# Computing the chosen two of eight experts, with rows sorted by expert through memory

## The reference, cut to what matters

```python
gate = softmax(flat_x @ w_gate.T)                    # flat_x = layernorm(x)
topk_scores, topk_idx = top_k(gate, 2)               # of 8 experts
cw = (one_hot(topk_idx, 8) * topk_scores[..., None]).sum(axis=1)
h = gelu(einsum('td,edh->teh', flat_x, W1) + b1)     # 128 -> 512, exact gelu
y = einsum('teh,ehd->ted', h, W2) + b2               # 512 -> 128
out = einsum('ted,te->td', y, cw)                    # x = x + 0.5 * out
```

## Time and profile before

| | us |
|---|---|
| median of 3 runs (range) | 2918.71 (2918.47 to 2922.16) |
| the profiled execution, its own time | 2922.81 |
| its span, first to last instruction | 2921.0 |
| busy: PE, DVE, ACT, POOL | 2432.8, 2039.1, 1732.1, 880.6 |

### The profile page before, as it was taken

How to read it: one execution, slowest core, us unless ns; L and a number is a source line. 1 busy time by engine, 2 the same in 40 slices (tenths; PEclk the granted TensorE clock), 3 DMA queues, 4 the chain that set the end, 5 groups by cost and what they waited for, 6 DMA issues and landing times. The chain is left out here.

```text
span 2921.0 us, 55825 instructions
## 1 busy us (share of the span) xinstructions
PE 2432.8 (83%) x17750; PEld 1732.7 (59%) x17878; DVE 2039.1 (70%) x3370; ACT 1732.1 (59%) x3364; POOL 880.6 (30%) x590
## 2 busy tenths in 40 slices
PE   5999997689999937888788888787688879788878
PEld 3767764267767725666446666443566655566654
DVE  5887876667887837888457888344688845788844
ACT  4767674167767725666465666457566646566646
POOL 1222221012222205444115444110444421444411
PEclk8999998889999968999899999889899979899989
DMA  3010111010110121101001111000101100111001
GB/s 118 29 58 29 40 47 59 0 58 30 29 58 29 32 95 27 26 22 26 4 4 25 26 24 26 1 3 0 23 22 26 24 10 0 23 26 26 22 8 29
DMA packets 51706, 84.66 MB, mean 29 GB/s; under 512 B 8574, under 2 KB 15144, under 8 KB 51640
## 3 DMA queue, kind: packets, MB, share of 16 engines
q1 hardware_dynamic: 49560, 77.79, 9.6%
q0 software_dynamic: 1216, 4.20, 0.5%
q10 hardware_dynamic: 864, 1.84, 0.2%
HBM read 51.59 MB, written 2.39 MB: 18 GB/s over the span
## 5 line engine op out<-in xcount | busy, mean ns | idle before, releaser
L384 ACT ACTIVATE moe_g<-banks,b 128x512 f32<-128x512 f32 x512 | 348.2, 691 | 242.5 <-PE banks L42 228.8
L481 DVE TENSOR_TENSOR moe_gl<-moe_g,moe_gh 128x512 fp32r<-128x512 f32 x512 | 397.6, 793 | 111.9 <-ACT moe_gh L388 103.1
L1287 POOL TENSOR_TENSOR att_sums<-att_turned 128x1024 f32<-128x1024 f32 x128 | 302.8, 2365 | 368.5 <-DVE att_turned L1178 337.7
L1178 DVE TENSOR_TENSOR att_turned<-banks,tables 128x512 f32<-128x512 f32 x512 | 317.5, 683 | 44.2 <-ACT att_squares L1080 44.2
L1294 POOL TENSOR_TENSOR att_qkn<-att_sums,att_rc 128x1024 f32<-128x1024 f32 x128 | 243.9, 1906 | 266.6 <-DVE att_rc L1193 230.2
L1109 ACT ACTIVATE att_probs<-banks,att_nmax 128x128 f32<-128x128 f32 x1024 | 289.1, 375 | 14.7 <-DVE att_nmax L1203 14.7
L1203 DVE TENSOR_REDUCE att_nmax<-banks 128x4 f32<-128x512 f32 x256 | 175.3, 686 | 139.1 <-PE banks L994 132.8
L509 POOL TENSOR_TENSOR moe_acc<-moe_acc,moe_part 128x512 f32<-128x512 f32 x96 | 153.5, 1598 | 376.5 <-DVE moe_part L457 376.5
L40 PE MATMUL banks<-wqkv_h,att_hh 128*128 128x512 f32 x384 | 179.2, 467 | 103.1 <-DVE att_qt L1198 66.1
L40 PE MATMUL banks<-moe_gh,w2h 128*128 128x512 f32 x512 | 214.0, 418 | 31.3 <-DVE moe_gl L481 30.8
L40 PE MATMUL banks<-moe_xh,w1h 128*128 128x512 f32 x512 | 221.3, 432 | 20.3 <-DVE moe_xl L447 20.3
(11 more groups left out here) (232 smaller groups left out, 5656.2 us busy)
## 6 DMA issues: line engine op xcount, KB each, us to landing
moe_cwb<-cw_dram SPq DMA_DIRECT2D x144, 256.0 KB, 4.5
att_v_even<-att_v SPq DMA_DIRECT2D x224, 130.0 KB, 2.3
raw_w<-in_L_ffn_W POOLq DMA_DIRECT2D x4, 512.0 KB, 9.8
raw_w<-in_L_ffn_W POOLq DMA_DIRECT2D x8, 256.0 KB, 12.5
out<-out_tokens SPq DMA_DIRECT2D x8, 256.0 KB
raw_qkv<-in_L_ffn_wqkv SPq DMA_DIRECT2D x2, 768.0 KB, 6.6
tables<-in_rotary ACTq DMA_DIRECT2D x2, 512.0 KB
raw_gated_w<-in_L_ffn_w SPq DMA_DIRECT2D x2, 341.0 KB, 8.0
```

What stands on the lines that cost most here:

```text
L384: act.activation(g32[:, s, :], m.ps[:, UP[i % len(UP)], :], ACT.Gelu, bias=w.b1[:, i:i + 1]).then_inc(gelu_done, 1)
L481: dve.tensor_tensor(gl[:, s, :], g32[:, s, :], gh[:, s, :], ALU.subtract).then_inc(lo_done, 1)
L1178: turn = dve.tensor_tensor(turned[:, i, k, :].rearrange("q (h s j) -> q h s j", s=2, j=DH // 2), q[:, :, ::-1, :] if i else q, table.unsqu ...
L1287: pool.tensor_tensor(sums[:], turned[:, 0, :, :], turned[:, 1, :, :], ALU.add).then_inc(added, 1)
```

## The change

`moe_phase` is replaced by three phases in a row. `dispatch_phase` runs layernorm, logits and ranking for all 8 blocks, ranks each token-expert choice within its expert by small matmuls against a triangle of ones, turns the normalised tokens to one token per partition, and scatters each token row twice (once for each chosen expert) into `x_sorted` in memory, with 64 indirect transfers of 128 rows of 512 bytes that POOL issues. It ends with a table: for each tile of 128 sorted rows its expert and its first row. `experts_phase` walks 72 tiles in 9 rounds of 8: SP fetches the rows, PE turns them, and now a tile's tokens are the stationary operand and the hidden units the moving one, so `up` is three 512-column matmuls for a tile; DVE adds the bias (it lies along columns now), ACT applies gelu, PE turns the result in four pieces, ACT and DVE split it, `down` is four 256-column, four 128-column matmuls and one that adds b2, DVE writes y and SP stores it at a row that a register holds. The experts' weights are addressed by registers, which `held` reads from the table on PE, DVE and SP. `combine_phase` gathers each token's two rows with 64 indirect transfers from POOL, DVE weighs and adds them, PE turns them back, DVE adds them to x. `load_phase` also writes zeros over `x_sorted`'s spare rows and over all of `y_sorted` (35840 rows of 512 bytes, 18.35 MB, in five transfers), and spreads b1 over the partitions (2.1 MB). The phases of `ssm_phase` and later are unchanged.

```diff
+NTOK = NB * T
+TOP = 2
+TOP_ROWS = TOP * NTOK
+NTILE = 72
+FILL = 5
+GROUP = 4
+NTAB = NTILE + 2 * GROUP
+SPARE = NTAB - TOP_ROWS // P
+REGION = NTOK + P
+ROWS = NE * REGION + SPARE * P
...
+            sp.wait_ge(blanked, 3)
+            sp.dma_start(x_sorted[NE * REGION:, :].rearrange("(s p) d -> p s d", p=P), m.blank[:].unsqueeze(1).to_broadcast([P, SPARE, P])).then_inc(spare_out, 16)
+            for k in range(2):
+                sp.dma_start(raw_b2[32 * k:32 * k + 1, :], consts["b2_flat"]).then_inc(b2_in, 16)
+            sp.dma_start(w.b1[:], consts["b1_flat"].to_broadcast([P, NE * T])).then_inc(rest_in, 16)
+            wide = y_sorted.rearrange("(p f c r) d -> f p c (r d)", p=P, f=FILL, r=NB)
+            for f in range(FILL):
+                sp.dma_start(wide[f], m.x[:, NTOK:].unsqueeze(1).to_broadcast([P, ROWS // P // FILL // NB, 2 * T])).then_inc(m.y_blank, 16)
             sp.wait_ge(consts_in, 32)
-            sp.wait_ge(rest_in, 64)
+            sp.wait_ge(rest_in, 80)
+            sp.wait_ge(spare_out, 16)
...
-def moe_phase(nc, m, app, w, cw_dram):
...
+def held(nc, engine, table, lo, n, top):
+    return nc.values_load_multi_w_load_instructions(
+        table[0:1, bass.ds(lo, n)], engines=(engine,), min_val=0, max_val=top,
+        skip_runtime_bounds_check_because="the table is made of counts that the shapes bound")[1]
...
+    WAYS, XBUF = 2, 3
+    LB, XB, PB = 4, [5, 6], 7
...
+            for b in range(NB + 3):
+                if b < NB:
+                    lns[b % WAYS].centre(pe, b // WAYS, m.x[:, b * T:(b + 1) * T])
+                if 1 <= b <= NB:
+                    lns[(b - 1) % WAYS].variance(pe, (b - 1) // WAYS)
+                if 2 <= b <= NB + 1:
+                    tokens(b - 2)
+                if b >= 3:
+                    ranks(b - 3)
...
+                step(dve.tensor_tensor(pos[:], p3, base[:].unsqueeze(1).to_broadcast([P, TT, NE]), ALU.add))
+                dve.tensor_tensor(base[:], m.ps[:, PB, TT * NE:(TT + 1) * NE], base[:], ALU.add).then_inc(placed, 1)
+                step(dve.tensor_tensor(got[:], picked[:], pos[:].unsqueeze(1).to_broadcast([P, TOP, TT, NE]), ALU.mult))
+                step(dve.tensor_reduce(place[:], got[:], AX.X, ALU.add))
+                dve.tensor_copy(route.index[:, n, :, :], place[:]).then_inc(indexed, 1)
...
+            for b in range(NB + 3):
+                if 1 <= b <= NB:
+                    if b - 1 >= 2:
+                        dve.wait_ge(xt_turned, START + b - 2)
+                    lns[(b - 1) % WAYS].norm(dve, (b - 1) // WAYS, xn[:, (b - 1) % 2, :])
+                if 2 <= b <= NB + 1:
+                    gates(b - 2)
+                if b >= 3:
+                    positions(b - 3)
+                if 2 <= b <= NB + 1:
+                    select(b - 2)
+            table()
...
+            for n in range(NB):
+                pool.wait_ge(xt_kept, START + n + 1)
+                pool.wait_ge(indexed, START + n + 1)
+                for t in range(TT):
+                    for k in range(TOP):
+                        pool.indirect_dma_start(
+                            x_sorted[:, :], bass.IndirectOffsetOnAxis(ap=route.index[:, n, k, t:t + 1], axis=0),
+                            xt[:, n % XBUF, t, :], None).then_inc(scattered[n % XBUF], 16)
...
+            def up(i, q, e):
+                if q % GROUP == 0:
+                    pe.wait_ge(split, START + 2 * i + q // GROUP + 1)
+                pe.wait_ge(biased, START + ROUND * i + q - 1)
+                cols = bass.ds(e * T, T)
+                flat = lambda t: t[:].rearrange("p e t -> p (e t)")[:, cols]
+                k, t = q // GROUP, q % GROUP
+                mm3(pe, m.ps[:, UB[q % 2], :], (xh[:, k, t, :], xl[:, k, t, :]),
+                    (flat(w.w1h), flat(w.w1l))).then_inc(up_done, 1)
+            def turn_g(i, q):
+                pe.wait_ge(gelued, START + ROUND * i + q + 1)
+                pe.wait_ge(gl_done, START + ROUND * i + q - 1)
+                for k in range(HC):
+                    tr = pe.transpose(m.ps[:, GB[q % 2], k * P:(k + 1) * P], g[:, q % 2, k, :], m.ident[:])
+                tr.then_inc(g_turned, 1)
+            def down(i, q, e):
+                pe.wait_ge(gl_done, START + ROUND * i + q + 1)
+                pe.wait_ge(y_done, START + ROUND * i + q - 1)
+                bank = m.ps[:, YB[q % 2], :]
+                flat = w.w2[:].rearrange("p e k s d -> p (e k s d)")
+                for k in range(HC):
+                    at = lambda n: flat[:, bass.ds(e * (HC * 2 * P) + k * 2 * P, n)]
+                    pe.matmul(bank[:, :2 * P], gh[:, q % 2, k, :], at(2 * P), start=k == 0, stop=False)
+                    pe.matmul(bank[:, :P], gl[:, q % 2, k, :], at(P), start=False, stop=False)
+                pe.matmul(bank[:, :P], m.ones_r[:], w.b2[:, bass.ds(e * P, P)], start=False, stop=True).then_inc(down_done, 1)
+            def round_of(i, first=False):
+                es = held(nc, mybir.EngineType.PE, route.owner, ROUND * i, ROUND + GROUP, NE - 1)
+                for q in range(ROUND):
+                    up(i, q, es[q + GROUP])
+                    if q == 1:
+                        turn_x(i, 1)
+                    if q == GROUP + 1:
+                        turn_x(i, 2)
+                    if q >= 1 or not first:
+                        turn_g(i, q - 1)
+                    if q >= 2 or not first:
+                        down(i, q - 2, es[q - 2 + GROUP])
...
+            def gelu(i, q):
+                act.wait_ge(biased, START + ROUND * i + q + 1)
+                act.wait_ge(g_turned, START + ROUND * i + q - 1)
+                act.activation(g[:, q % 2, :, :].rearrange("p k d -> p (k d)"), pre[:, q % 2, :], ACT.Gelu).then_inc(gelued, 1)
+            def upper(i, q):
+                act.wait_ge(g_turned, START + ROUND * i + q + 1)
+                act.wait_ge(down_done, START + ROUND * i + q - 1)
+                act.activation(gh[:, q % 2, :, :].rearrange("p k d -> p (k d)"), m.ps[:, GB[q % 2], :],
+                               ACT.Copy).then_inc(gh_done, 1)
...
+            def bias(i, q, e):
+                dve.wait_ge(up_done, START + ROUND * i + q + 1)
+                dve.wait_ge(gelued, START + ROUND * i + q - 1)
+                dve.tensor_tensor(pre[:, q % 2, :], m.ps[:, UB[q % 2], :], w.b1[:, bass.ds(e * T, T)], ALU.add).then_inc(biased, 1)
+            def lower(i, q):
+                dve.wait_ge(gh_done, START + ROUND * i + q + 1)
+                dve.tensor_tensor(gl[:, q % 2, :, :].rearrange("p k d -> p (k d)"), m.ps[:, GB[q % 2], :],
+                                  gh[:, q % 2, :, :].rearrange("p k d -> p (k d)"), ALU.subtract).then_inc(gl_done, 1)
+            def keep_y(i, q):
+                dve.wait_ge(down_done, START + ROUND * i + q + 1)
+                dve.wait_ge(y_out[q % GROUP], START + 16 * (2 * i + q // GROUP))
+                dve.tensor_copy(y[:, q % GROUP, :], m.ps[:, YB[q % 2], :P]).then_inc(y_copied, 1)
+                dve.wait_ge(y_copied, START + ROUND * i + q + 1)
+                dve.tensor_tensor(y[:, q % GROUP, :], m.ps[:, YB[q % 2], P:2 * P], y[:, q % GROUP, :], ALU.add).then_inc(y_done, 1)
+            def round_of(i, first=False):
+                es = held(nc, mybir.EngineType.DVE, route.owner, ROUND * i + GROUP, ROUND, NE - 1)
+                for q in range(ROUND):
+                    bias(i, q, es[q])
+                    if q == 1:
+                        keep_x(i, 1)
+                    if q == GROUP + 1:
+                        keep_x(i, 2)
+                    if q >= 1 or not first:
+                        lower(i, q - 1)
+                    if q >= 2 or not first:
+                        keep_y(i, q - 2)
...
+            with sp.Fori(0, NR) as b:
+                at = rows_of(ROUND * b, 2 * ROUND)
+                for k in range(2):
+                    sp.wait_ge(x_turned, START + 2 * b + k + 1)
+                    load(b, k, at[ROUND + k * GROUP:ROUND + (k + 1) * GROUP])
+                    for q in range(k * GROUP, (k + 1) * GROUP):
+                        store(b, q, at[q])
...
+            for n in range(NB):
+                if n >= YBUF:
+                    pool.wait_ge(summed, START + TT * (n - YBUF + 1))
+                for t in range(TT):
+                    for k in range(TOP):
+                        pool.indirect_dma_start(
+                            yg[:, n % YBUF, k, t, :], None, y_sorted[:, :],
+                            bass.IndirectOffsetOnAxis(ap=route.index[:, n, k, t:t + 1], axis=0)).then_inc(y_in[n % YBUF], 16)
...
+        dispatch_phase(nc, m, app, w, route, x_sorted)
+        experts_phase(nc, m, app, w, route, x_sorted, y_sorted)
+        combine_phase(nc, m, app, route, y_sorted)
```

More of the change, by code:

```diff
@@ L299, in moe_phase @@
-        wchain = sem("wchain")
-        cw_in = [sem(f"cw_in{e}") for e in range(NE)]
-        GSTEPS = 8
+        picked, chosen = sb("picked", [P, TOP, TT, NE]), sb("chosen", [P, TT, NE], BF16)
```

(70 more changed lines are left out.)

453 lines of the change are left out of this document (236 added, 217 removed).

## The result

| | time, us (median) | against the kernel before |
|---|---|---|
| before, same chip | 2920.4 | |
| changed | 2956.2 (2955.3 to 2963.2, 4 runs) | 1.0127, 95% interval 1.0108 to 1.0146 |
| changed, once more, in the third group of runs (`e15_changed_again`) | 2986.4 (2982.8 to 2990.1, 4 runs) | 1.0221, 1.0204 to 1.0238 |

What follows compares the result with a forecast made beforehand. The prediction took PE to bound the old mixtures. It added 13 us for the two new mixtures and 27 us for loading, +40 us on the median 2918.7, giving 2959 us, range 2850 to 3065.

Steps and rivals of the forecast that it cites:

- Indirect transfers: Dispatch and combine: POOL's issue bounds at 1.0 us for each of 256 transfers, bounds 0.76 to 1.37.
- cheap indirect transfers: Rival, dispatch and combine: a transfer costs 0.76 us, saving 61 us, total 2898; chance 0.15.
- Period of a tile: Experts phase: a serial chain over DVE and ACT sets 3.8 us a tile, 274 us for 72 tiles.
- clock term: Experts phase: PE at half clock 12% of the time, at a mean clock of 0.942, adds 0.13 us a tile.
- The reads: Experts phase: DVE's eight register reads at a round's start, 0.25 us each, 2 us a round, 0.25 a tile.
- the base: Experts phase: bias, gelu, upper, lower and keep_y in series with hops take 3.25 us a tile.
- chain free of reads and clock: Rival, experts phase: period 3.43 us a tile, 53 us less, total 2906; chance 0.15.
- Loading: Loading phase: zero transfers hold SP's queue, the phase ends with SP at 56, 27 us longer.
- Boundaries: Phase ends in each mixture: four of 2.8 us where the old windows had two, 11.2 us together.
- PE as the bound: Rival, experts phase: half clock throughout, period 4.8 us, 144 us more, total 3103; chance 0.10.
- POOL starved by DVE: Rival, dispatch: half of the 128 scatters doubled beside DVE's work, 64 us more, total 3023; chance 0.10.
- SP held to the end: Rival, loading: SP held until the zeros end, 19 to 40 us over the forecast, 2978 to 2999; chance 0.08.

Runs made afterwards that it cites:

- e15_changed_again: The changed kernel without an edit, run once more in the third group: 2986.4 us, 1.0221 against the kernel before.
- e4: Changed kernel with the combine issuing only each token's first-expert gathers, leaving out 32 of 64 in each of two combines: 2873.5 us.
- e12: Changed kernel with one more gather, of 16 rows instead of 128, behind each of a combine's 64: 3148.1 us.
- e2: Changed kernel with ScalarE's round issuing upper(q-1) ahead of gelu(q) instead of behind it: 2867.9 us, 0.9829 against the kernel before.
- e5: Changed kernel with up issuing one matmul a tile instead of three, without the two products with the lower halves: 2991.1 us, second group.
- e13: Changed kernel with VectorE reading a round's eight expert numbers in eight loads of one value, not one load of eight: 3027.5 us, third group.
- e3: Changed kernel with the five zero transfers to y_sorted issued when the first dispatch begins, not ahead of the other loads: 2936.0 us, 1.0060 against the kernel before.
- e11_read_twice: Changed kernel with a second, unused read of DVE's expert numbers, absent from the program, so it served as the second group's changed kernel: 2982.4 us.

## Why the prediction was right, and where it was not

**The sum was right by two errors of opposite sign.** That the total came out within 3 us of the forecast is luck. For the first mixture, forecast and measured in the changed kernel's own trace, both with the boundaries:

| | forecast | measured | difference |
|---|---|---|---|
| boundary ahead | 2.8 | 2.5 (55.1 to 57.6) | -0.3 |
| dispatch | 85.2 | 103.2 (to 160.8: last scatter issued at 158.6, landed 2.2 later) | +18.0 |
| boundary | 2.8 | 7.5 (to 168.3) | +4.7 |
| experts and boundary | 292.4 | 253.2 (to 421.5) | -39.2 |
| combine | 70.5 | 85.1 (to 506.6) | +14.6 |
| boundary behind | 2.8 | 2.8 (to 509.4) | 0 |
| sum | 456.5 | 454.3 | -2.2 |

**Indirect transfers.** The mechanism held: POOL issues almost without a break, DVE is done with the table at 132.1 and 27 us of POOL alone follow (e4: 83 us for 64 gathers less). The term of 1.0 for each transfer was mis-sized: it is 0.96 and 0.94 busy plus 0.30 between two, which the nearest row, a direct transfer with idle 0.0 ahead, did not show. That is 16 to 18 us in each of four phases, 66 in all. 1.25 lies in the stated bounds, 0.76 to 1.37. The rival *cheap indirect transfers* is refuted; so is the argument for it, the number of pieces, since rows hardly count (e12).

**Period of a tile.** The mechanism held here too: the list of DVE, gelu and upper between bias and lower. e2 took gelu out from in front of upper on ACT, with PE's work unchanged, and gave 88 us; in e5 a PE with fewer matmuls at a lower clock left the wait in front of lower as it was. The size was 3.8 against 3.29, some 37 us a mixture. Three parts of it: the clock term was 0.13 and is 0, since 0.99 was granted; in e5, with two of up's three matmuls gone, it was 0.77, and even that cost only 0.05 a tile. The reads were 2.0 us a round by 0.25 for each of eight; the boundary costs 0.90, because they are one load of 0.60 (e13). The Trainium skill ("Runtime: NRT & Kernel Launch", Instruction fetch mechanics) has about 200 ns per register for loads from HBM, by which eight are an estimated 1.6 us. The 0.60 measured here from on-chip memory is well under it, and a load of one value, 0.30, is over it; the measurement decides. The rest is the base: from lower to lower 2.99 in the timeline against the forecast 3.25, since bias to lower takes 1.86, where 0.69, 0.63 and 0.60 with hops had been added up in full. PE's own bill, 2.4 us a tile in the prediction, was too low as well: it is busy for 197.8 us in 72 tiles, 2.75 each, and holds the period at 2.71 in e2. Under DVE's chain that did not count. The rival *chain free of reads and clock* (3.43, 2906) was thus more than right on the period and wrong on the total.

**Loading.** Right: SP's queue was held to 55.1 (56 forecast), the phase 25.7 longer (27). e3 shows the cause, with 20 us given back, and that the bytes themselves cost 2 us at most under the dispatch.

**Boundaries.** Three of the four are as forecast; between dispatch and experts it is 7.5 and not 2.8 after the last landing, and no view shows what is waited for in it.

**PE as the bound** (half clock throughout) did not happen: 0.99 was granted, and in e5, at 0.77, the period was still 3.35 and not 4.8. **POOL starved by DVE**: POOL's scatters took 0.96 in the window with DVE busy 36.9 of 53 us and 0.95 in the window where it did nothing (21.86 us in 23 instructions). The Trainium skill ("SBUF — State Buffer", SBUF: two separate sides) has about 3100 ns in place of 620 for a transfer beside DVE work in a two-port mode. With this DVE work no trace here shows that: the longest of the 64 took 1.20 us. The rival's 3023 was not reached; in the two later groups DVE is late with an index, through stalls, in dispatches that are 8 to 11 us longer. **SP held to the end** did not happen.

**Open.** What the stalls are that PE, DVE and POOL have in the dispatch of the two later groups; why the boundary behind the scatters is 7.5 us, and why that behind the gathers is 2.8 in the first trace, 5.0 in `e11_read_twice` and `e15_changed_again` and 16.1 in e12. They are in or behind the stages with indirect transfers and not in the experts phase; no run takes them apart from these. A dispatch with half its scatters was not tried.

## What to carry to other kernels

Routing work away from the bounding engine pays only if the issue of the transfers is cheap: here 256 indirect DMAs at 1.25 us took back 320 of the 430 us that 72 tiles in place of the dense loop had saved over both mixtures, and their price is one of the instruction, so use all 128 partitions in each. When three engines hand a tile round, write down whose list puts what in front of what before sizing anything: two calls exchanged on ACT were worth 88 us. A large write that nobody needs soon belongs behind the loads, on a queue that no one waits for at that time.

## What the runs showed of the hardware

- An indirect DMA of 128 rows of 512 bytes is busy on POOL for 0.94 to 0.96 us and the next starts 0.30 later; with 16 rows it is 0.86 and 0.30 (e12).
- A register load from on-chip memory on DVE: 0.30 us for one value (e13), 0.60 for eight.
- TensorE was granted 0.99 of its 2.4 GHz in the experts phase (busy for 197.8 of 234.0 us), and 0.77 when two of `up`'s three matmuls had been taken out of the same phase (e5, busy for 208.4 of 238.1 us).
- Five zero transfers of 3.58 MB in a row held SP's queue for 30.1 us in the load phase, and for 26.5 us beside the dispatch (e3).
- The kernel before took 2920 to 2923 in every group; the changed one took 2956 in its first runs and 2982 to 2986 in the second and third group.
